# Order of scans, gatings and transposes in a four-layer stack on one core

## What is computed

```
num, den = both-way scans over time of exp(k)*v and exp(k) with a decay
y   = sigmoid(x) * (num / max(den, 1e-8)) * (0.8 + 0.2*tf)
x   = x + FFN_layer(y)
L0: rmsnorm, int8 quantization per token; gate, up, down with ternary weights; SiLU
L1: router, top 2 of 8 experts, each gelu(y @ w1 + b1) @ w2 + b2
L2: integer weights with scales: silu(gate) * up, then down
L3: layernorm, blockwise 8-bit quantization (32 along the channels), W1, tanh GELU,
    blockwise quantization, W2, all rounded to bf16
```

## Time and profile before

| | us |
|---|---|
| three runs | 435.94, 436.25, 438.63; median 436.25 |
| the profiled execution | 436.66 |
| its span, first to last instruction | 434.9 |
| TensorE products busy | 382.7 (88%) |
| VectorE busy | 343.7 (79%) |
| ScalarE busy | 287.3 (66%) |
| GpSimd busy | 93.6 (22%) |
| mean granted TensorE clock | 0.969 of 2.4 GHz |

### The profile page before, as it was taken

The page is one execution under the profiler, slowest core; times in us unless marked ns, Lnnn a source line. Parts: engine busy times, 40 slices in busy tenths (PEclk is TensorE's granted clock), DMA queues, the critical chain, the costliest instruction groups (busy, mean ns, idle before and its releaser), DMA issues.

```text
span 434.9 us, 7332 instructions
## 1 busy us (share of the span) xinstructions
PE 382.7 (88%) x2627; PEld 327.2 (75%) x2627; DVE 343.7 (79%) x507; ACT 287.3 (66%) x508; POOL 93.6 (22%) x103
## 2 busy tenths in 40 slices
PE   2998677399796889999999999999999987999896
PEld 2998654177784469999999999999986776788444
DVE  4999978789566899999999990499504786799885
ACT  5996975278987177767676767576643454778854
POOL 4000010200012044344442513256630000000000
PEclk9999988599899799999999999999999999999999
DMA  7700000000017562831152168583004200000011
GB/s 273 238 0 2 2 2 0 0 2 0 2 16 279 193 223 91 286 128 39 36 167 102 36 230 296 178 249 114 24 14 134 85 0 2 0 2 0 2 37 62
DMA packets 22691, 38.55 MB, mean 89 GB/s; under 512 B 2088, under 2 KB 17080, under 8 KB 22528
## 3 DMA queue, kind: packets, MB, share of 16 engines
q1 hardware_dynamic: 17120, 24.98, 17.0%
q0 software_dynamic: 2528, 7.08, 4.9%
q10 hardware_dynamic: 3008, 6.03, 4.2%
HBM read 32.97 MB, written 5.11 MB: 88 GB/s over the span
## 4 chain that ended last, share of the span: by engine, by line
PE 61%; DVE 21%; ACT 8%; issue 6%; DMA 2%; POOL 1%; ACTq 1%; SPq 0%; DVEq 0%
PE bank L1749 19%; PE bank L1727 18%; PE bank L1812 4%; PE bank L1584 3%; PE bank L1555 2%; PE bank L1802 2%; DVE scr L862 2%; DVE scr L864 2%; PE bank L1615 2%; PE bank L1858 1%; DVE big L1247 1%; PE bank L1719 1%; PE bank L1602 1%; DMA v<-in_kT 1%; DMA g<-choice_rows 1%
## 5 line engine op out<-in xcount | busy, mean ns | idle before, releaser
L1727 PE MATMUL bank<-big,yT 128*128 x368 | 83.3, 379 | 0.0
L617 ACT ACTIVATE yT<-bank,big 128x128 f32<-128x128 f32 x184 | 52.5, 369 | 42.7 <-PE bank L1749 41.2
L1727 PEld LDWEIGHTS bank<-big,yT 128*128 128x128 f32 x368 | 68.1, 190 | 8.8 <-issue 0.4
L374 POOL TENSOR_TENSOR small<-small 128x2 f32<-128x2 f32 (+1 forms) x9 | 9.7, 1073 | 180.0 <-DVE small L1282 74.6
L422 POOL DMA_INDIRECT choice_rows<-yo,rowo x23 | 32.6, 1417 | 63.4 <-ACT yo L626 44.7
L407 POOL DMA_INDIRECT xg<-token_rows,rowi x23 | 32.9, 1432 | 50.5 <-PE bank L1719 30.6
L1555 PE MATMUL bank<-identf,scr 128*128 128x128 f32 x240 | 31.5, 292 | 3.8 <-DVE scr L875 3.8
L1555 PEld LDWEIGHTS bank<-identf,scr 128*128 128x128 f32 x240 | 30.6, 209 | 4.1 <-DVE scr L875 4.0
L1749 PEld LDWEIGHTS bank<-ygT,big 128*128 128x128 f32 x256 | 29.8, 192 | 1.9 <-issue 1.6
L1749 PE MATMUL bank<-ygT,big 128*128 128x128 f32 x256 | 29.9, 275 | 1.4 <-ACT ygT L609 1.4
L1749 PEld LDWEIGHTS bank<-ygT,w3T 128*128 128x128 f32 x256 | 29.7, 192 | 1.6 <-issue 1.3
(11 more groups left out here) (368 smaller groups left out, 815.5 us busy)
## 6 DMA issues: line engine op xcount, KB each, us to landing
big<-in_moe_w SPq DMA_DIRECT2D x16, 1024.0 KB
v<-in_kT SPq DMA_DIRECT2D x2, 512.0 KB, 4.7
big<-in_gateT SPq DMA_DIRECT2D x1, 1024.0 KB, 7.2
big<-in_upT SPq DMA_DIRECT2D x1, 1024.0 KB, 9.3
big<-in_downT SPq DMA_DIRECT2D x1, 1024.0 KB, 11.7
x<-in_x_bsc SPq DMA_DIRECT2D x1, 1024.0 KB, 14.0
token_rows<-y POOLq DMA_DIRECT2D x4, 256.0 KB, 7.6
ek<-in_w3a ACTq DMA_DIRECT2D x1, 1024.0 KB, 7.8
```

Source lines behind the costliest of these rows:

```text
L617: ins = sc.activation(hT[j % 2][:, c], ps[1 + 2 * (j % 2) + c // 4][:, (c % 4) * P:(c % 4 + 1) * P], ACT.Gelu, bias=b1s[:, c, j:j + 1])
L1727: ins = te.matmul(ps[5 + 2 * (j % 2)][:, 0:C], hT[j % 2][:, c], big[:, bass.ds(at + (W2_AT + c * C), C)], start=(c == 0), stop=(c == IC - 1))
```

## The change

It edits only orders, with the waits and banks that belong to them; every product, scan and copy stays but for the fillers. In the head of layer 0, ScalarE squares before it makes the third ternary weight and quantizes four tiles before the inversion of n = 2 and the other four ahead of the SiLU table load; VectorE moves n = 2's backward denominator scan behind the maxima, and its gv, floor and numerator scans behind the token statistic, the scales and the first copies. In the four passes, VectorE's scans of n = 2 and 3, the floors, the ratio and the second half of a Newton step stand later, between the gatings of passes 1 to 3; TensorE's `add_up` parts and ScalarE's decay follow them. In layers 2 and 3 the transposes of x for pair 3 move to pass 1, the norm transposes of a pair to the end of its own pass, the second up product of a pass behind all gate products; ScalarE loads the sigmoid's table ahead of the norm copy; one gating of pair 0 goes between two sums. In the tail, transposes of tiles 4 to 6 use banks 1 and 2, tile 4's stand ahead of the last norm's, the last tile's first half ahead of tile 6's down product, and the fillers fall from 47 products to 29.

```diff
   if p == 0:
-    turns += [f"x{q}" for q in range(1, G)]
+    turns += ["x1", "x2"]
+  elif p == 1:
+    turns += ["x3"]
...
 last_bank = (ps[6], ps[3])
+turn_bank = [ps[6]] * (T - 4) + [ps[1], ps[2], ps[1]]
...
   euk(3)
-  ternary(2)
...
     sc.activation(squares0[i], y0t[:, i], ACT.Square, accum_out=ss[:, i:i + 1]).then_inc(s["stat_sq"], 1)
-  invert(2)
-  sc.preload_act_table(ACT.Silu)
+  ternary(2)
...
   for i in range(T):
+    if i == T // 2:
+      invert(2)
...
            scale=kq[:, i:i + 1]).then_inc(s["q_magic"], 1)
-  decay_of(3)
+  sc.preload_act_table(ACT.Silu)
...
     silu(b)
-    if p == T // 2 - 1:
-      sc.preload_act_table_set("natural_log_exp_and_others")
...
     square(b)
+    if p == T // 2 - 1:
+      sc.preload_act_table_set("natural_log_exp_and_others")
...
       evict(b - 2)
+    if p == 1:
+      decay_of(3)
...
       act.wait_ge(s["d3_ready"], i - 1)
-    sc.activation(q3T[i % 2], ps[6][:].bitcast(BF16).rearrange("p (c t) -> p c t", c=HC3),
+    sc.activation(q3T[i % 2], turn_bank[i][:].bitcast(BF16).rearrange("p (c t) -> p c t", c=HC3),
...
   for p in range(G):
-    if p >= 2:
-      copy_hqT(p - 2)
...
       sigmoid_l3(p - 1)
-    if p == 1:
-      sigmoid_l2(3)
-    if p >= 1:
...
     silu_l2(p, 1)
-    if p >= 2:
-      copy_u3(2 * p - 3)
...
       gelu_l3(2 * p - 4)
+      copy_u3(2 * p - 3)
...
       gelu_l3(2 * p - 3)
-    if p == 1:
-      head_y2(3)
-    if p >= 3:
-      copy_q3T(2 * p - 5)
-      copy_ob(2 * p - 6)
...
       head_y2(2)
-  copy_hqT(G - 2)
+    else:
+      if p == 1:
+        sigmoid_l2(3)
+      copy_hqT(p - 1)
+      if p == 1:
+        head_y2(3)
+    if p >= 3:
+      copy_ob(2 * p - 6)
+      copy_q3T(2 * p - 5)
   sigmoid_l3(G - 1)
+  copy_u3(T - 4)
+  sc.preload_act_table(ACT.Gelu_apprx_tanh)
+  gelu_l3(T - 4)
   copy_ob(T - 7)
-  sc.preload_act_table(ACT.Gelu_apprx_tanh)
-  copy_u3(T - 4)
-  gelu_l3(T - 4)
...
   copy_ob(T - 5)
+  copy_q3T(T - 4)
...
   gelu_l3(T - 1)
-  copy_q3T(T - 4)
...
   copy_q3T(T - 2)
+  copy_last(0)
   copy_ob(T - 2)
-  copy_last(0)
...
   clamp(3)
-  sweep(2, True)
+  sweep(2, True, back=False)
...
             apply_absolute_value=True).then_inc(s["stat_max"], 1)
-  make_gv(2)
-  sweep(2, False, back=False)
+  sweep(2, True, back=True)
...
   ve.tensor_scalar(ss, ss, 1.0 / C, 1e-6, ALU.mult, ALU.add).then_inc(s["stat_tok"], 1)
-  floor_ps(2)
+  make_gv(2)
...
   ve.tensor_tensor(kq[:], kq[:], r_[:], ALU.mult).then_inc(s["scale_ready"], 1)
-  sweep(2, False, back=True)
+  floor_ps(2)
...
   q0T_of(1)
+  sweep(2, False, back=False)
...
   q0T_of(3)
-  link(ve.scalar_tensor_tensor(dc[0], dc[0], 2.0, r0[2], ALU.subtract, ALU.mult))
...
     gate_z(a)
-    if p == 0:
+    if p >= 2:
+      add_down(dve, ve, a - 4)
+      add_down(dve, ve, a - 3)
+    if p == 1:
+      sweep(2, False, back=True)
+    elif p == 2:
+      sweep(3, True, back=False)
+    elif p == 3:
+      floor_n3(0)
+      sweep(3, False, back=False)
+    gate_z(b)
+    amax_z(a)
+    amax_z(b)
+    if p == 1:
...
       ins.then_inc(s["num_used"], 1)
-    if p >= 2:
-      add_down(dve, ve, a - 4)
-      add_down(dve, ve, a - 3)
-    gate_z(b)
-    amax_z(a)
-    amax_z(b)
-    if p == 1:
-      make_gv(3)
     elif p == 2:
+      sweep(3, True, back=True)
+    elif p == 3:
+      floor_n3(1)
...
     if p == 0:
-      sweep(3, True, back=False)
-    elif p <= 2:
-      floor_n3(p - 1)
+      link(ve.scalar_tensor_tensor(dc[0], dc[0], 2.0, r0[2], ALU.subtract, ALU.mult))
+    elif p == 1:
+      make_gv(3)
...
     ve.tensor_tensor(kq[:, c], kq[:, c], r_[:, c], ALU.mult).then_inc(s["scale2"], 1)
-    if p == 0:
-      sweep(3, True, back=True)
-    elif p == 1:
-      sweep(3, False, back=False)
...
       dve.wait_ge(s["bias_added"], p + 1)
+      if i == 5:
+        gate_l2(0, 2)
...
   combine(2)
-  gate_l2(0, 2)
...
   norm_max(0)
-  scale_y2(3)
   norm_exp(0)
+  gate_l2(1, 2)
   norm_unit(0)
-  gate_l2(1, 2)
...
   norm_scaled(0)
-  rest_y2(3)
...
   norm_quant(0)
+  scale_y2(3)
+  rest_y2(3)
...
   pe.wait_ge(s["num_used"], 1)
-  for part in range(3):
+  for part in range(2):
...
       pe.wait_ge(s["x_l0"], 2 * (i // 2))
+    elif i == 0:
+      pe.wait_ge(s["w_ternary"], 3)
...
   turn_y0(1)
-  pe.wait_ge(s["w_ternary"], 3)
+  pe.wait_ge(s["w_ternary"], 2)
...
   gate_up(0, 1)
-  add_up(2, 2, 3, False, tuple(range(T)))
...
   gate_up(1, 1)
+  add_up(2, 2, 2, False, tuple(range(T)))
...
     if p == 1:
-      pe.wait_ge(s["num_used"], 3)
-      add_all(3, 3, True, low)
-    elif p == 2:
+      add_up(2, 2, 3, False, tuple(range(T)))
+    elif p == 3:
...
       add_all(3, 3, True, high)
-    else:
-      pe.wait_ge(s["n3_taken"], 2)
-      add_up(3, 3, 0, False, low)
-      add_up(3, 3, 1, False, low)
...
       gate_up(a + 2, 1)
-    else:
-      add_up(3, 3, 2, False, low)
-      add_up(3, 3, 3, False, low)
+    if p == 1:
+      pe.wait_ge(s["num_used"], 3)
...
     down(b - 2)
+    if p == 2:
+      add_all(3, 3, True, low)
+    elif p == 3:
+      pe.wait_ge(s["n3_taken"], 2)
+      for part in range(4):
+        add_up(3, 3, part, False, low)
...
     pe.wait_ge(s["hq3"], p + 1)
-    if p >= 1:
+    if p == 1:
       pe.wait_ge(s["hq3T"], p)
-    if p >= 2:
-      pe.wait_ge(s["q3T_ready"], 2 * p - 2)
+    elif p >= 2:
+      pe.wait_ge(s["q3T_ready"], 2 * p - 3 if p < G - 1 else T - 4)
...
     pe.wait_ge(s["q3_ready"], i + 1)
-    if i % 2 == 0 and i // 2 + 2 <= G:
-      pe.wait_ge(s["hq3T"], i // 2 + 2)
-    else:
+    if i == 0:
+      pe.wait_ge(s["hq3T"], 2)
+    elif i == 1:
+      pe.wait_ge(s["hq3T"], 3)
+    elif i < T - 4:
       pe.wait_ge(s["q3T_ready"], i)
+    elif i == T - 2:
+      pe.wait_ge(s["q3T_ready"], T - 3)
     for c in range(HC3):
-      ins = te.transpose(ps[6][:].bitcast(BF16)[:, c * P:(c + 1) * P], q3[i % 2][:, c * P:(c + 1) * P], identb[:])
+      ins = te.transpose(turn_bank[i][:].bitcast(BF16)[:, c * P:(c + 1) * P], q3[i % 2][:, c * P:(c + 1) * P], identb[:])
...
     pe.wait_ge(s["q3_ready"], T + h)
-    pe.wait_ge(s["q3T_ready"], T - 1)
+    pe.wait_ge(s["hq3T"], G)
...
   for p in range(G):
-    if p >= 2:
-      norm_to_channels(p - 2)
...
     gate_up_l2(p, 1, 1)
-    if p >= 2:
-      up_l3(2 * p - 3)
...
       x_to_channels(1)
+    elif p == 1:
+      x_to_channels(3)
+    else:
+      up_l3(2 * p - 3)
...
       x_to_channels(2)
+    else:
+      norm_to_channels(p - 1)
     if p >= 3:
+      down_l3(2 * p - 6)
       turn_l3(2 * p - 5)
-      down_l3(2 * p - 6)
     down_l2(p, 1)
-    if p == 0:
-      x_to_channels(3)
-    if p >= 3:
-      down_l3(2 * p - 5)
-  norm_to_channels(G - 2)
-  keep_clock(0, 3)
   up_l3(T - 4)
-  keep_clock(0, 3)
+  down_l3(T - 7)
...
   turn_l3(T - 6)
-  keep_clock(0, 3)
+  keep_clock(0, 9)
+  down_l3(T - 6)
   turn_l3(T - 5)
-  down_l3(T - 6)
...
   down_l3(T - 5)
+  turn_l3(T - 4)
+  norm_to_channels(G - 1)
+  keep_clock(0, 3)
+  up_l3(T - 2)
+  down_l3(T - 4)
+  up_l3(T - 1)
+  turn_l3(T - 3)
   keep_clock(0, 10)
-  norm_to_channels(G - 1)
+  down_l3(T - 3)
   keep_clock(0, 4)
-  up_l3(T - 2)
-  keep_clock(0, 3)
-  up_l3(T - 1)
-  turn_l3(T - 4)
-  keep_clock(0, 6)
-  down_l3(T - 4)
-  turn_l3(T - 3)
-  keep_clock(0, 6)
-  down_l3(T - 3)
   turn_l3(T - 2)
-  keep_clock(0, 6)
+  turn_last(0)
   down_l3(T - 2)
-  turn_last(0)
```

## The result

The changed kernel took 430.66 us (median of 4 runs, 428.04 to 432.05) beside 436.10 of the kernel before (4 runs): ratio 0.9862, interval 0.9833 to 0.9891. Timed again on another occasion, unaltered, it gave 430.84 and 0.9872 (0.9826 to 0.9918). So it is 1.3 to 1.4% faster, over the 1% that can be told. I had forecast 428 with a range of 424 to 434: 2.7 too much gain. An execution over 1.5% above the fastest of its kernel is left out of the ratios and medians here.

The account below looks back on a forecast made before the run. No engine is full in layer 0's gated stage; engines wait for one another in a hand-written order. 436.66 − 5.0 (layer 0) − 3.4 (last two layers) = 428.3, say 428 us; range 424 to 434 for 8 in 10.

Parts of the forecast that it names:

- VectorE's first gating starts at 64.1: Head of layer 0: first gating at 64.1 instead of 69.32, 5.2 us earlier, following the first SiLU's end at 63.8.
- the term 5.0 for layer 0: Layer 0: 5.2 us gained in the head less 0.4 in the passes, taken as 5.0; bounds nothing to 8.
- Of the table load all 1.28 is on the path now: Head of layer 0: ScalarE's SiLU table load, its cover nearly gone, delays the first SiLU by its full 1.28 us.
- The passes: Layer 0's four passes on VectorE: 10.4, 12.8, 12.6 and 13.9 us, sum 49.7, 0.4 more than before.
- Rival (b): Layer 0's passes give back the head's gain because gatings wait for TensorE after the scans: 433.8 us; chance 0.12.
- Rival (c): Slower: TensorE stays at half clock through layer 0's gated stage: 445.9 us at 85% of its work; chance 0.05.
- The power: GpSimd's power in passes 0 and 1 waits out a two-input VectorE product of 1.2 us, ending 0.6 behind it.
- the bound of 1.2 below: Layer 0's passes: their sum would be 1.2 us lower if the power did not wait out the two-input product.
- The last two layers: Layers 2 and 3 with the tail: 3.4 us gained at the last output copy; bounds 0 and 4.5.
- Rival (a): The last two layers give nothing, a down product standing behind ScalarE's queue in pass 3: 431.7 us; chance 0.13.
- The fillers: Tail: falling from 47 to 29 they cost nothing; without them TensorE idles at most 1.3 us at a time.
- Rival (d): The tail, with fewer fillers, falls to half clock and products on the path double: 432.8 us; chance 0.03.

Follow-up runs that it names:

- c_gv: c_pe2 with make_gv(2), a two-input product, moved off GpSimd's power to behind floor_ps(2): 427.12 us, ratio 0.9792.
- c_pe2: Changed kernel with n = 2's numerator part 0 ahead of denominator part 3 and numerator part 1 behind gate_up(1, 1) on TensorE: 427.49 us, ratio 0.9807.
- b_only: Kernel before with only the edits of layers 2 and 3, layer 0 left as before: 433.52 us, ratio 0.9942.
- e_hq: Changed kernel with ScalarE's norm copy ahead of the sigmoid's table load in passes 2 and 3: 428.24 us (3 runs), ratio 0.9813.
- e_nofill: Changed kernel without the tail's 29 filler products: 435.11 us, ratio 0.9944.
- t_late: Changed kernel with tile 4's turn and the last tile's first half late again, as before, fillers kept: 433.58 us, ratio 0.9928.
- c_clk: c_pe2 with 42 filler products added in layer 0 beside TensorE's waits: 428.79 us, ratio 0.9795.
- best: c_gv plus e_hq's edit, timed beside the unaltered changed kernel (430.84 us) on one chip: 425.60 us, ratio 0.9752.

## Why the prediction was right, and where it failed

**The step that failed:** "VectorE's first gating starts at 64.1", 5.2 earlier; it came at 66.48, 2.84 earlier, and with it the term 5.0 for layer 0 was 2.96. Two things are in it.
- First quantization 56.61, not 55.65. ScalarE was free at 55.0, near my 55.4, but the power of eight columns took 2.56 beside the gv product, where I had let the gv product cover it and counted on the old chain of 3.22; the chain took 4.4. I had applied the waiting-out to passes 0 and 1 and not here. c_gv shows 1.12 us for it.
- I followed ScalarE to its table load and stopped there. On TensorE, 48 identity products stood ahead of the token transposes, the first 16 at half clock behind a wait of 6.22. The prediction goes from the quantization straight to the first SiLU and never adds up this queue. c_pe2 shows 1.7 us at the gating for 32 of them.

"Of the table load all 1.28 is on the path now" was wrong too: ScalarE was past it at 64.0, made one SiLU and waited 3.39.

**The passes** were right in sum, in part because their misses cancel (0.9 over in pass 0, 0.5 and 0.6 under in passes 2 and 3): 11.3, 12.7, 12.1, 13.3, together 49.4, against 49.7 forecast from 10.4, 12.8, 12.6 and 13.9. Pass 0 is over by 0.9 with most of its twelve gate products at half clock (4.51 us); in c_pe2, where all twelve ran at full clock, it took 10.42. TensorE's wait in pass 1 was 4.04 for my "near 4"; the products behind it stayed at half clock (3.57), as before. Rival (b) did not happen: behind the scan of pass 1 one gating waited 0.95 for a SiLU that had waited for TensorE, behind those of pass 3 none. Rival (c) neither: clock 0.92.

**The power** waits out a two-input product: 1.60 against 0.70, as I had chosen; the bound of 1.2 below does not hold. The Trainium skill, "SBUF — State Buffer", section "Who interferes with whom", has this rule, and the trace agrees in passes 0 to 3. In the head the same rule would have told me of the 1.0 that I missed in the quantization.

**The last two layers** gave 3.58 for 3.4, and each step on the way was right to 0.4 us. Counted from the bias product (its start 2.63 earlier): x of pair 0 0.9 earlier (forecast 0.9), of pair 1 1.79 (1.7), of pair 2 3.15 (2.8), of pair 3 0.85 (0.8), the last quantization 2.2 (1.9), the last copy 3.58 (3.4). Behind the last quantization 2.15 were needed and not 1.9, which the 0.3 more ahead of it made good. Rival (a) fell by b_only. The copy behind the table load gave back 2.3 (3.15 less 0.85), for the 2.0 forecast; e_hq, which moved the copy ahead of the load, took 1.43 of it away. The Trainium skill, "ScalarE: Activation LUTs", section "What ACT_TABLE_LOAD costs", gives 2.66 us for a switch, a drain included; here the load takes 1.28 and the next instruction starts 1.30 behind it.

**The fillers** were the other wrong sentence, though not in the sum: I priced their absence at nothing; it is 5.2, since TensorE then stands idle for 2.92 us, not 1.3. Rival (d)'s mechanism is real, but 29 of 47 were enough that the clock stayed 1.00 in the tail. That they kept it was not worked out beforehand; there I was lucky.

**The size.** The sum foresaw 8.4 us and the profiles show 6.2; the 2.0 that layer 0 fell short are nearly all of it. By the ratios on record the two halves timed alone give 0.6 (−0.7 to 2.0) and 2.5 us (1.1 to 4.0), together 3.1, and the whole 5.6 to 6.0 (4.8 to 7.6). By the medians they give 1.4 and 3.4, together 4.8, against 5.4 and 5.3 for the whole. So much of the gap depends on how the middle is taken, and the intervals allow the rest; in the profiles the halves (2.7 to layer 0's end, 3.50) do add to 6.2. Nothing here shows that one half needs the other.

## What to carry to other kernels

When one engine's work is moved forward, write down the whole queue of every engine that the result must pass, with each instruction's length at half clock if an idle stretch lies ahead of it; the transfer of a gain stops at the first in-order queue that was not reordered with it. A product that nobody waits for belongs behind one that somebody waits for, and the price can be more than its length: here 32 products, 3.9 us at full clock, cost 1.7 at the gating, and 2.0 more behind it where waits were longer and the products after them slow. Fillers are set for one order: after a change count them again, for too few (5.2 us in e_nofill) and for too many on the path (1.8 us in t_late).

## What was not expected of the hardware

- The same layer 0 code ended at 126.27 and 126.48 in two executions of one kernel and at 124.61 in another kernel, with the granted clock of 64 to 68 us at 0.57, 0.57 and 1.00. TensorE had waited 2.08, 2.08 and 1.23 us for the quantization just before. The length of that wait does not settle it: c_gv and best have the same code in layer 0 too, and the gate products behind 64.2 us ran at full clock in c_gv, after waits of 1.97 and 1.24 us, and at half in best, after 1.61 and 0.97. What decides stays open; it goes with 1.0 to 1.9 us at the end of the stage, so a gain of that size can't be read from two profiles.
- In the tail, TensorE's clock fell to 0.53 some 1 us behind the end of an idle time of 2.92 us; with fillers, which cut that idle time to 0.98, it stayed at 1.00. In t_late it idled 2.72 us, and the products behind that, fillers among them, still ran at full clock (1.05 and 1.04 for eight of a down product).
- Forty-two fillers beside TensorE's waits raised the mean clock of layer 0's stage only from 0.96 to 0.97 (c_clk against c_pe2), and the stage ended 0.27 us later. Twenty-nine of them in a tail of 30 us were worth 5.2.
